# Graph convolutions and first experts: products wait for the tile or half of the columns they read, not for the whole stage before

## The chip, the cores and the metric

One core of one Trainium2 chip runs the whole program. Its engines are TensorE (PE, matmuls into PSUM banks, with weight loads PEld beside them), VectorE (DVE), ScalarE (ACT), GpSimd (POOL) and SyncE (SP, which issues transfers). Each runs its own list of instructions in order, and they wait for one another through counting semaphores. The metric is the device time of one execution in microseconds.

## What is computed

A two-layer network of a graph and token mixture: 625 nodes with 768 features, 20,000 edges. The change touches two parts of layer 0: two graph convolutions, and a mixture of eight small experts with the two best chosen for each node.

```python
# graph convolution, twice (a relu between)
h = x @ W
out = segment_sum(h[src] * (dinv[src] * dinv[dst])[:, None], dst) + b
# first experts: hidden width 192 each, top 2 of 8
hidden = gelu(einsum("ecd,edh->ech", padded, w1) + b1, approximate=False)
out    = einsum("ech,ehd->ecd", hidden, w2) + b2
final  = zeros.at[pt].add(out[se, pos] * pw[:, None])
```

Behind them come an attention of a second kind, a graph attention and the large experts, which the change doesn't touch.

## The kernel before, in words

**Precision.** Every float32 product is made of three matmuls (`mm3`, lines 341 to 343): an operand is a pair of an upper half, which ScalarE makes (`upper`, line 359), and a lower half, which VectorE makes from it (`lower`, line 362). Each pair counts on a semaphore once its lower half is there. So a stage hands over like this: TensorE fills a bank, ScalarE reads it and writes the upper half, VectorE writes the lower half, and TensorE may read the pair.

**Sizes.** The 625 nodes stand in `TT` = 5 tiles of `P` = 128; `D` = 768 columns are `KD` = 6 blocks of 128, and two halves of `HALF` = 384. Where nodes are the columns of a product they are cut into `SPANS` = (0, 320) and (320, 306).

**Banks.** `ring.next(...)` hands out the eight PSUM banks in turn, and makes TensorE wait for the eviction of what stood in that bank eight products earlier.

**Graph convolutions** (`graph_convolutions`). The edges have been counted into a dense matrix `adj` of 625 x 625. Per layer TensorE makes

- ten *node products* `node(layer, n)` with `c, t = divmod(n, TT)`: tile t of x times column half c of W, six terms, 18 matmuls of 384 columns. The result is the pair `h`; its lower half counts on `h_lo` ("node_lo"). All five tiles of half 0 come before those of half 1;
- in layer 1 twelve *neighbour products*, m over six blocks of 128 columns of h and s over the two spans: five terms, 15 matmuls of 320 or 306 columns. ScalarE adds bias and relu, and the pair goes to `xT`, counted on `z_lo` ("hidden_lo");
- in layer 2 ten *sums*, tile t outside and half c inside, 15 matmuls of 384 columns each, which VectorE adds to x. After tile t VectorE and ScalarE normalise it, and TensorE transposes tile t - 1 (`turn_tensor`).

The matrix `adj` itself is scaled tile by tile during the node products of layer 1; its lower halves count on `adj_lo`.

**First experts** (`dense_experts`). The hidden layer of all experts (1536) is made in two halves kh of twelve *hidden units*, each one block of 128 hidden numbers by one span: units 0 to 2 of a half are span 0 of its first three blocks, 3 to 5 span 1 of them, 6 to 8 span 0 of the last three blocks, 9 to 11 span 1. With each unit goes a short product of two matmuls, the gates' rows (lines 354 and 355). ScalarE applies gelu, VectorE multiplies by the gate, ScalarE and VectorE split the result into the pair `hT`, counted on `h_lo` ("hidden_lo"). Then come ten *sums* over the six blocks: 21 matmuls each in half 0 (with a bias term), 18 in half 1. In half 0 all tiles of c = 0 come first, in half 1 tile t stands outside and c inside.

At each of the five hand-overs TensorE had one wait for the last lower half of the stage:

```python
pe.wait_ge(*h_lo.at(2 * TT))        # before the neighbour products
pe.wait_ge(*z_lo.at(2 * KD))        # before the node products of layer 2
pe.wait_ge(*h_lo.at(4 * TT))        # before the sums
pe.wait_ge(*h_lo.at(12 * (kh + 1))) # experts: before the sums of each half
```

Of the kernel before, what the change touches and what calls it, by code (L numbers as in the profile page):

```python
# [17 lines left out]
P = 128  # L18
T = 625
TT = (T + P - 1) // P  # L20
# [4 lines left out]
KD = D // P  # L25
HALF = D // 2
# [36 lines left out]
SPANS = [(0, 320), (320, 306)]  # L63
# [7 lines left out]
class Signal:  # L71
# [20 lines left out]
    def at(self, n):  # L92
        return self.semaphore, self.base + n
# [48 lines left out]
def tok(t):  # L142
    return slice(t * P, (t + 1) * P)
# [11 lines left out]
def program(nc, ins, out, slots_dram, ctx):  # L155
    pe, act, dve, pool, sp = nc.tensor, nc.scalar, nc.vector, nc.gpsimd, nc.sync
# [95 lines left out]
    def buffers(i):  # L252

        n = width[i]
        if slot[i] == DEPTH:
            return tuple(part[:, 0:n] for part in fifth)
        return raw[:, slot[i], 0:n], whi[:, slot[i], 0:n], wlo[:, slot[i], 0:n]
# [74 lines left out]
    def weight(*key):  # L332

        i = place[key]
        pe.wait_ge(w_lo.semaphore, i + 1)
        k = TERMS.get(key[0], KD)
        return tuple(w.rearrange("p (k n) -> p k n", k=k) for w in buffers(i)[1:])
# [646 lines left out]
    def graph_convolutions(xT_ready):  # L984
# [24 lines left out]
        def tensor():  # L1009
            def node(layer, n):  # L1010
                c, t = divmod(n, TT)
                w = weight(f"gnn0_w{layer}", c)
                bank = ring.next(h_lo.at(2 * TT * (layer - 1) + n + 1))
                h_banks.append(bank)
                product(bank[:, 0:HALF], [(at(xT, ALL, k, tok(t)), at(w, ALL, k, ALL)) for k in range(KD)]).then_inc(*h_full.one())

            pe.wait_ge(*xT_ready)
            for n in range(4):
                node(1, n)
            pe.wait_ge(*adj_lo.at(1))  # L1020
            pe.wait_ge(*ones_made.now())
            for i, (a0, n) in enumerate(((0, 320), (320, 320))):
                bank = ring.next(deg_kept.at(i + 1))
                deg_banks.append(bank)
                product_exact_a(bank[0:E, 0:n], [(ones[:, 0:E], at(adj, ALL, k, slice(a0, a0 + n))) for k in range(TT)]).then_inc(*deg_full.one())
            node(1, 4)
            pe.wait_ge(*deg_kept.at(2))
            bank = ring.next(deg_root.at(1))
            deg_banks.append(bank)
            for t in range(TT):  # L1030
                end = pe.transpose(bank[:, t * E:(t + 1) * E], deg_row[:, tok(t)], ident[0:E, 0:E])
            end.then_inc(*deg_full.one())
            node(1, 5)
            pe.wait_ge(*deg_inv.at(1))
            for i, (t0, n) in enumerate(SPREAD):
                bank = ring.next(looped.at(2 * TT))
                deg_banks.append(bank)
                for k in range(n):
                    end = pe.transpose(bank[:, k * P:(k + 1) * P], deg_col[:, t0 + k:t0 + k + 1].broadcast_to([P, P]), ident[:, :])
                end.then_inc(*deg_full.one())  # L1040
            for n in range(6, 2 * TT):
                node(1, n)
            pe.wait_ge(*h_lo.at(2 * TT))
            pe.wait_ge(*adj_lo.at(1 + TT))
            for m in range(KD):
                for s, (a0, n) in enumerate(SPANS):
                    bank = ring.next(z_relu.at(2 * m + s + 1))
                    z_banks.append(bank)
                    product(bank[:, 0:n], [(at(h, ALL, k, slice(m * P, (m + 1) * P)), at(adj, ALL, k, slice(a0, a0 + n)))
                                           for k in range(TT)]).then_inc(*z_full.one())  # L1050
            pe.wait_ge(*z_lo.at(2 * KD))
            for n in range(2 * TT):
                node(2, n)
            pe.wait_ge(*h_lo.at(4 * TT))
            for t in range(TT):
                for c in range(2):
                    bank = ring.next(y_added.at(2 * t + c + 1))
                    y_banks.append(bank)
                    product(bank[:, 0:HALF], [(at(adj, ALL, k, tok(t)), at(h, ALL, k, slice(c * HALF, (c + 1) * HALF)))
                                              for k in range(TT)]).then_inc(*y_full.one())  # L1060
                if t > 0:
                    norm.turn_tensor(t - 1)
# [189 lines left out]
    def dense_experts(norm, x_ready):  # L1252
# [9 lines left out]
        m = sb("ffn0_m", [P, 2, TT], F32, scope)  # L1262
# [52 lines left out]
        def tensor():  # L1315
            def logits():
                pe.wait_ge(*gate_lo.at(1))
                pe.wait_ge(*xT_ready[-1])
                for s, (a0, n) in enumerate(LOGIT_SPANS):
                    bank = ring.next(logits_kept.at(s + 1))  # L1320
                    logit_banks.append(bank)
                    product(bank[0:E, 0:n], [(at(gp, ALL, k, ALL), at(xT, ALL, k, slice(a0, a0 + n))) for k in range(KD)]).then_inc(*logits_full.one())

            def logits_turned():
                pe.wait_ge(*logits_kept.at(2))
                bank = ring.next(logits_kept.at(3))
                logit_banks.append(bank)
                for t in range(TT):
                    end = pe.transpose(bank[:, t * E:(t + 1) * E], logit_rows[:, tok(t)], ident[0:E, 0:E])
                end.then_inc(*logits_full.one())  # L1330

            def counts_turned():
                pe.wait_ge(*count_f_made.at(TT))
                for t in range(TT):
                    for k0, kn in PARTS:
                        bank = ring.next(count_kept.at(len(count_banks) + 1))
                        count_banks.append(bank)
                        for k in range(kn):
                            end = pe.transpose(bank[:, k * P:(k + 1) * P], count_f[:, k0 + k, tok(t)], ident[:, :])
                        end.then_inc(*count_turned.one())  # L1340

            def hidden(i):
                hid, _, span, n = unit(i)
                w = weight("ffn0_w1", i // 6)
                pe.wait_ge(*xT_ready[-1 if i % 6 // 3 else (SPANS[0][1] - 1) // P])
                bank = ring.next(gelu.at(i + 1))
                hid_banks.append(bank)
                mm = hid % 3
                product(bank[:, 0:n], [(at(w, ALL, k, slice(mm * P, (mm + 1) * P)), at(xT, ALL, k, span)) for k in range(KD)]).then_inc(*hid_full.one())

            def picked(i):
                hid, _, span, n = unit(i)
                bank = ring.next(gated.at(i + 1))
                pick_banks.append(bank)
                product_exact_a(bank[:, 0:n], [(sel[:, hid, :], at(gT, ALL, span))]).then_inc(*pick_full.one())

            hidden(0)
            norm.turn_tensor(TT - 1)
            hidden(1)
            hidden(2)  # L1360
            logits()
            hidden(3)
            logits_turned()
            hidden(4)
            hidden(5)
            counts_turned()
            gates_tensor(gates, gate_banks)
            hidden(6)
            pe.wait_ge(*gT_lo_made.at(TT))
            pe.wait_ge(*sel_made.at(1))  # L1370
            for i in range(EARLY):
                picked(i)
            for kh in range(2):
                for i in range(max(EARLY, 12 * kh), 12 * (kh + 1)):
                    hidden(i)
                    picked(i)
                pe.wait_ge(*h_lo.at(12 * (kh + 1)))
                pe.wait_ge(*b2_lo.at(1))
                for i, (t, c) in enumerate(SUMS[kh]):
                    w = weight("ffn0_w2", 2 * kh + c)  # L1380
                    cols = slice(c * HALF, (c + 1) * HALF)
                    n = ROWS[t]
                    rows = slice(t * P, t * P + n)
                    bank = ring.next(y_added.at(2 * TT * kh + i + 1))
                    y_banks.append(bank)
                    terms = [(at(hT, ALL, k, rows), at(w, ALL, k, ALL)) for k in range(HK)]
                    if kh == 0:
                        terms.append((at(gT, ALL, rows), at(b2p, ALL, cols)))
                    product(bank[0:n, 0:HALF], terms).then_inc(*y_full.one())
                    if kh == 1 and c == 1 and t > 0:  # L1390
                        norm2.turn_tensor(t - 1)
# [1985 lines left out]
```

## Time and profile before

| | us |
|---|---|
| median of 3 runs | 1967.06 (1966.3 to 1967.81) |
| the profiled execution | 1970.35 |
| its span | 1968.5 |
| TensorE busy with matmuls | 1850.9 (94% of the span) |
| VectorE busy | 1292.1 (66%) |
| ScalarE busy | 934.7 (47%) |
| layer 0's graph convolutions, in the span | about 313 to 438 |
| its experts, in the span | about 438 to 605 |

Times in the rows are microseconds from the start of the span. TensorE's matmuls are pipelined: the time between two starts is what a matmul costs, not its duration, which is longer. The granted clock of TensorE is a share of 2.4 GHz; 0.50 is its lower level, 1.2 GHz. Idle time of an engine is followed by the instruction whose end released it. The chain of work that ended last runs over TensorE for nearly all of its length that is put down to an engine (43% of the span against 3% for VectorE).

### The profile page before, as it was taken

How to read it: one execution, taken by the hardware profiler on the slowest of the kernel's cores; microseconds unless marked ns; L12 is line 12 of the kernel's file. 1: busy time of each engine (PE TensorE's matmuls, PEld its weight loads, DVE VectorE, ACT ScalarE, POOL GpSimd, SP SyncE). 2: the span in 40 equal slices, each digit the busy share in tenths (PEclk: the TensorE clock that was granted, in tenths of full speed). 3: DMA queues.
4: the chain of work that ended last, by engine and by line, in shares of the span. 5: the costliest groups of instructions: out<-in, count | busy, mean ns of one | idle time of the engine just before them, and what ended most of it. 6: DMA issues, size and time to landing. Idle time of an engine off the chain costs nothing.

```text
span 1968.5 us, 30877 instructions
## 1 busy us (share of the span) xinstructions
PE 1850.9 (94%) x12157; PEld 1753.9 (89%) x12158; DVE 1292.1 (66%) x2489; ACT 934.7 (47%) x1547; POOL 150.5 (8%) x127
## 2 busy tenths in 40 slices
PE   6987999999999999788789999999999999999998
PEld 5876789998899999787689999999999999999998
DVE  7997766555245556888865754456566667676886
ACT  2331223315125435878534232345555566666776
POOL 0000000003000022333100000000101001001010
PEclk9997999999999989899799999999999999999999
DMA  3110002101113112010131132255656567677795
GB/s 117 49 49 1 25 25 105 54 6 71 49 49 110 54 36 95 22 38 17 64 123 61 62 105 73 73 208 181 220 193 221 214 217 242 219 260 250 282 318 203
DMA packets 36844, 234.30 MB, mean 119 GB/s; under 512 B 5964, under 2 KB 7366, under 8 KB 14680
## 3 DMA queue, kind: packets, MB, share of 16 engines
q1 hardware_dynamic: 31366, 217.41, 31.1%
q0 software_dynamic: 2656, 8.99, 2.1%
q10 hardware_dynamic: 2674, 5.87, 0.8%
q8 instruction: 99, 1.62, 0.3%
q14 instruction: 49, 0.40, 0.1%
HBM read 221.91 MB, written 10.35 MB: 118 GB/s over the span
## 4 chain that ended last, share of the span: by engine, by line
PE 43%; issue 3%; DVE 3%; DMA 1%; ACT 1%; POOL 0%; ACTq 0%; POOLq 0%; DVEq 0%
PE bank L2755 8%; PE bank L341 7%; PE bank L342 7%; PE bank L343 7%; PE bank L2756 4%; PE bank L2767 3%; PE bank L2771 2%; PE bank L2759 2%; PE bank L2768 2%; PE bank L2770 1%; PE bank L2758 1%; DVE weight_lo L314 1%; DMA out<-ffn_y,slot_token 0%; PE bank L2713 0%; DMA weight_raw_fifth<-in_ffn_w 0%
## 5 line engine op out<-in xcount | busy, mean ns | idle before, releaser
L314 DVE TENSOR_TENSOR weight_lo<-weight_raw,weight_hi 128x2304 fp32r<-128x2304 f32 (+1 forms) x155 | 392.3, 2536 | 51.5 <-ACT weight_hi L304 51.4
L304 ACT ACTIVATE weight_hi<-weight_raw 128x2304 fp32r<-128x2304 f32 (+1 forms) x155 | 323.3, 2087 | 76.7 <-DMA weight_raw<-in_ffn_w 55.0
L341 PE MATMUL bank<-xT_hi,weight_hi 128*128 128x320 f32 (+1 forms) x576 | 183.2, 318 | 5.3 <-DVE xT_lo L362 5.2
L342 PE MATMUL bank<-xT_lo,weight_hi 128*128 128x320 f32 (+1 forms) x576 | 178.3, 310 | 0.0
L343 PE MATMUL bank<-xT_hi,weight_lo 128*128 128x320 f32 (+1 forms) x576 | 178.1, 309 | 0.0
L341 PE MATMUL bank<-weight_hi,xT_hi 128*128 128x384 f32 (+1 forms) x480 | 161.2, 336 | 11.2 <-DVE weight_lo L314 6.2
L3135 DVE TENSOR_TENSOR hidden_tmp<-hidden_tmp,bank 128x160 f32<-128x160 f32 (+5 forms) x192 | 65.6, 342 | 160.7 <-ACT hidden_tmp L2918 160.7
L342 PE MATMUL bank<-weight_lo,xT_hi 128*128 128x384 f32 (+1 forms) x480 | 157.0, 327 | 0.0
L343 PE MATMUL bank<-weight_hi,xT_lo 128*128 128x384 f32 (+1 forms) x480 | 156.7, 326 | 0.0
L613 PE MATMUL bank<-one_hot_dst,one_hot_src 125*128 125x313 f16 x800 | 123.5, 306 | 15.2 <-ACT packed_counts L627 7.9
L2918 ACT ACTIVATE hidden_tmp<-bank,ffn_b_by_load 128x160 f32<-128x160 f32 (+5 forms) x192 | 73.3, 402 | 117.5 <-PE bank L2759 112.8
L341 PE MATMUL bank<-weight_hi,hidden_hi 128*128 128x384 f32 (+1 forms) x366 | 124.6, 340 | 0.5 <-DVE weight_lo L314 0.5
L342 PE MATMUL bank<-weight_lo,hidden_hi 128*128 128x384 f32 (+1 forms) x366 | 123.8, 338 | 0.0
L613 PEld LDWEIGHTS bank<-one_hot_dst,one_hot_src 125*128 125x128 f16 x800 | 75.0, 100 | 52.4 <-DVE one_hot_dst L585 17.2
L2755 PE MATMUL bank<-xT_hi,weight_hi 128*128 128x512 f32 (+3 forms) x390 | 117.4, 361 | 3.4 <-DVE xT_lo L3090 1.7
L341 PEld LDWEIGHTS bank<-xT_hi,weight_hi 128*128 128x128 f32 x576 | 110.3, 192 | 10.6 <-issue 7.7
L343 PE MATMUL bank<-weight_hi,hidden_lo 128*128 128x384 f32 (+1 forms) x348 | 117.7, 338 | 0.0
L2755 PE MATMUL bank<-xT_lo,weight_hi 128*128 128x320 f32 (+3 forms) x390 | 110.5, 350 | 5.6 <-DVE xT_hi L3090 4.6
L342 PEld LDWEIGHTS bank<-xT_lo,weight_hi 128*128 128x128 f32 x576 | 110.6, 192 | 0.0
L343 PEld LDWEIGHTS bank<-xT_hi,weight_lo 128*128 128x128 f32 x576 | 110.4, 192 | 0.0
L341 PEld LDWEIGHTS bank<-weight_hi,xT_hi 128*128 128x128 f32 x480 | 93.1, 194 | 13.5 <-DVE weight_lo L314 7.0
L2756 PE MATMUL bank<-xT_hi,weight_lo 128*128 128x256 f32 (+3 forms) x390 | 97.7, 250 | 0.0
(495 smaller groups left out, 5040.8 us busy)
## 6 DMA issues: line engine op xcount, KB each, us to landing
weight_raw<-in_ffn_w SPq DMA_DIRECT2D x111, 1152.0 KB, 5.2
weight_raw_fifth<-in_ffn_w SPq DMA_DIRECT2D x25, 1152.0 KB, 5.2
weight_raw<-in_shared_w SPq DMA_DIRECT2D x16, 1152.0 KB, 5.1
weight_raw<-in_mix_kv SPq DMA_DIRECT2D x8, 1152.0 KB, 7.0
weight_raw<-in_gat_w SPq DMA_DIRECT2D x8, 768.0 KB, 4.3
weight_raw<-in_mix_q SPq DMA_DIRECT2D x4, 1152.0 KB, 5.1
weight_raw<-in_mix_out SPq DMA_DIRECT2D x4, 1152.0 KB, 5.2
weight_raw<-in_gnn_w SPq DMA_DIRECT2D x4, 1152.0 KB, 5.6
```

The costliest lines, as they stand in the source:

```text
L304: act.activation(upper_, whole_, ACT.Copy).then_inc(*w_hi.one())
L314: dve.tensor_tensor(lower_, whole_, upper_.bitcast(F32), ALU.subtract).then_inc(*w_lo.one())
L341: pe.matmul(dst, a[0], b[0], start=first, stop=False)
L342: pe.matmul(dst, a[0], b[1], start=False, stop=False)
L343: return pe.matmul(dst, a[1], b[0], start=False, stop=last)
L613: end = pe.matmul(edge_banks[t][:, 0:TM], hot_src[:, j % HOT, tok(t)], hot_dst[:, j % HOT, 0:TM], start=(i == 0), stop=(i == CHUNK_E - 1))
L2755: pe.matmul(both, hi[:, k, :], x_e[:, k, :, 0:width], start=(k == 0), stop=False)
L2756: pe.matmul(first, lo[:, k, :], x_e[:, k, 0, 0:width], start=False, stop=False)
L2759: end = pe.matmul(both, hi[:, k, :], x_e[:, k, :, 0:width], start=False, stop=True)
L2767: pe.matmul(both, hi[:, k, :], h[:, k, :, 0:width], start=(first and k == 0), stop=False)
L2918: act.activation(ht[:, i % 3, 0:CAPS[e]], r_banks[i][:, 0:CAPS[e]], ACT.Identity, bias=b1r[:, e, i % (3 * NCH):i % (3 * NCH) + 1]).then_in ...
L3135: dve.tensor_tensor(part, part, r_banks[i][:, width:2 * width], ALU.add).then_inc(*r_sum.one())
```

## The change

Five single waits become waits at the head of each product, on the count that this product's operands need:

```diff
@@ graph convolutions
-            pe.wait_ge(*h_lo.at(2 * TT))
             pe.wait_ge(*adj_lo.at(1 + TT))
             for m in range(KD):
+                pe.wait_ge(*h_lo.at(TT if (m + 1) * P <= HALF else 2 * TT))
                 for s, (a0, n) in enumerate(SPANS):
...
-            pe.wait_ge(*z_lo.at(2 * KD))
             for n in range(2 * TT):
+                pe.wait_ge(*z_lo.at(2 * KD - 1 if (n % TT + 1) * P <= SPANS[0][1] else 2 * KD))
                 node(2, n)
-            pe.wait_ge(*h_lo.at(4 * TT))
             for t in range(TT):
                 for c in range(2):
+                    pe.wait_ge(*h_lo.at((3 + c) * TT))
                     bank = ring.next(y_added.at(2 * t + c + 1))
...
@@ first experts
-                pe.wait_ge(*h_lo.at(12 * (kh + 1)))
                 pe.wait_ge(*b2_lo.at(1))
                 for i, (t, c) in enumerate(SUMS[kh]):
+                    pe.wait_ge(*h_lo.at(12 * kh + (9 if (t + 1) * P <= SPANS[0][1] else 12)))
                     w = weight("ffn0_w2", 2 * kh + c)
```

So the neighbour products of column blocks 0 to 2 ask for the node products of half 0 alone; node tiles 0 and 1 of layer 2, which lie inside the first span of 320, ask for step 11 of 12; the sums of half 0 of the columns ask for 15 of 20 node products; the experts' sums of tiles 0 and 1 ask for nine of twelve units.

No instruction moves on any engine. TensorE's matmuls stand in the same order, and 34 heads of products have one more wait. On TensorE, at the head of the third neighbour product (bank free of `deg` work: "loops_added"; "node_lo" is `h_lo`):

```order
 L342 MATMUL bank<-adj_lo,gcn_h_hi 128x306
 L343 MATMUL bank<-adj_hi,gcn_h_lo 128x306
-L341 MATMUL bank<-adj_hi,gcn_h_hi 128x320 [waits loops_added]
+L341 MATMUL bank<-adj_hi,gcn_h_hi 128x320 [waits loops_added,node_lo]
 L342 MATMUL bank<-adj_lo,gcn_h_hi 128x320
 L343 MATMUL bank<-adj_hi,gcn_h_lo 128x320
```

The first product's head has the same names before and after, with a lower count behind "node_lo"; the third has the wait anew. On TensorE, at the head of the experts' second sum of half 0 ("hidden_gated" is the bank's eviction, "weight_lo_made" the weights', "hidden_lo" the wait on `h_lo`):

```order
 L342 MATMUL bank<-ffn_b_lo,ffn_gatesT_hi 8x384
 L343 MATMUL bank<-ffn_b_hi,ffn_gatesT_lo 8x384
-L341 MATMUL bank<-weight_hi,ffn_hT_hi 128x384 [waits hidden_gated,weight_lo_made]
+L341 MATMUL bank<-weight_hi,ffn_hT_hi 128x384 [waits hidden_gated,weight_lo_made,hidden_lo]
 L342 MATMUL bank<-weight_lo,ffn_hT_hi 128x384
 L343 MATMUL bank<-weight_hi,ffn_hT_lo 128x384
```

A head that had two waits has three; the matmuls around it stand where they stood.

## Rows read from the trace of the kernel before

**Rows 1.** The page's first part: busy us, share of span, instructions.

```profile
PE 1850.9 (94%) x12157; PEld 1753.9 (89%) x12158; DVE 1292.1 (66%) x2489; ACT 934.7 (47%) x1547; POOL 150.5 (8%) x127
```

**Rows 2.** Waits of TensorE, whole span: us in total, times, longest.

```profile
PE bank L341 <- DVE ffn_hT_lo L362: 4.5, 2, 2.8
```

**Rows 3.** Timeline, TensorE, hand-over 1: start, duration, instruction, idle before.

```profile
344.53 0.34 PE L343 MATMUL bank<-weight_hi,xT_lo 128*128 128x384 f32 x1
346.04 0.42 PE L341 MATMUL bank<-adj_hi,gcn_h_hi 128*128 128x320 f32 x1 [1.17 <-DVE gcn_h_lo L362]
346.29 0.31 PE L342 MATMUL bank<-adj_lo,gcn_h_hi 128*128 128x320 f32 x1
```

**Rows 4.** Timeline, TensorE, hand-over 2.

```profile
371.89 0.30 PE L343 MATMUL bank<-adj_hi,gcn_h_lo 128*128 128x306 f32 x1
373.79 0.44 PE L341 MATMUL bank<-weight_hi,xT_hi 128*128 128x384 f32 x1 [1.61 <-DVE xT_lo L362]
```

**Rows 5.** Timeline, TensorE, hand-over 3, and the first transposes behind it.

```profile
404.76 0.33 PE L342 MATMUL bank<-weight_lo,xT_hi 128*128 128x384 f32 x1
404.93 0.34 PE L343 MATMUL bank<-weight_hi,xT_lo 128*128 128x384 f32 x1
406.44 0.45 PE L341 MATMUL bank<-gcn_h_hi,adj_hi 128*128 128x384 f32 x1 [1.17 <-DVE gcn_h_lo L362]
406.72 0.34 PE L342 MATMUL bank<-gcn_h_lo,adj_hi 128*128 128x384 f32 x1
...
416.96 0.81 PE L474 MATMUL bank<-identity,counts_with_loops 128*128 128x128 f32 x6
```

**Rows 6.** Stretches: us, busy of PE, PEld, DVE, ACT, POOL, clock, DMA, GB/s.

```profile
484.00:488.00 4.00, 2.70 (x9) 2.70 (x10) 1.94 (x3) 3.22 (x3) 0.00 (x0) 0.71 0.61 256
700.00:1100.00 400.00, 349.63 (x2258) 332.78 (x2257) 294.57 (x840) 232.41 (x470) 82.80 (x73) 0.91 0.16 56
```

**Rows 7.** Timeline, VectorE, before hand-over 1: the last tile of `adj_lo`.

```profile
342.93 0.82 DVE L362 TENSOR_TENSOR adj_lo<-counts_with_loops,adj_hi 128x640 fp32r<-128x640 f32 x1
```

**Rows 8.** Timeline, VectorE, before hand-over 2: step 11 of 12.

```profile
371.17 0.49 DVE L362 TENSOR_TENSOR xT_lo<-gcn_tmp,xT_hi 128x320 fp32r<-128x320 f32 x1 [0.87 <-ACT xT_hi L359]
```

**Rows 9.** Timeline, VectorE, behind hand-over 3: tile 0 normalised.

```profile
414.46 0.68 DVE L466 TENSOR_SCALAR counts_with_loops<-x,ln_moments,ln_rstd 128x768 f32<-128x768 f32 x1
```

**Rows 10.** Timeline, TensorE, hand-over 4, experts' first half.

```profile
479.03 0.30 PE L355 MATMUL bank<-ffn_gatesT_lo,expert_rows_r 8*128 8x306 f32 x1
479.26 0.41 PE L341 MATMUL bank<-xT_hi,weight_hi 128*128 128x306 f32 x1
479.50 0.30 PE L342 MATMUL bank<-xT_lo,weight_hi 128*128 128x306 f32 x1
...
482.23 0.30 PE L355 MATMUL bank<-ffn_gatesT_lo,expert_rows_r 8*128 8x306 f32 x1
485.30 0.44 PE L341 MATMUL bank<-weight_hi,ffn_hT_hi 128*128 128x384 f32 x1 [2.77 <-DVE ffn_hT_lo L362]
485.58 0.45 PE L342 MATMUL bank<-weight_lo,ffn_hT_hi 128*128 128x384 f32 x1
...
489.03 0.36 PE L341 MATMUL bank<-weight_hi,ffn_hT_hi 128*128 128x384 f32 x1
```

**Rows 11.** Timeline, VectorE, before hand-over 4: units 9 and 12.

```profile
480.38 0.49 DVE L362 TENSOR_TENSOR ffn_hT_lo<-ffn_acted,ffn_hT_hi 128x320 fp32r<-128x320 f32 x1 [0.61 <-ACT ffn_hT_hi L359]
...
484.77 0.48 DVE L362 TENSOR_TENSOR ffn_hT_lo<-ffn_acted,ffn_hT_hi 128x306 fp32r<-128x306 f32 x1 [0.59 <-ACT ffn_hT_hi L359]
```

**Rows 12.** Timeline, TensorE, hand-over 5, experts' second half.

```profile
566.54 0.30 PE L355 MATMUL bank<-ffn_gatesT_lo,expert_rows_r 8*128 8x306 f32 x1
568.56 0.44 PE L341 MATMUL bank<-weight_hi,ffn_hT_hi 128*128 128x384 f32 x1 [1.71 <-DVE ffn_hT_lo L362]
```

**Rows 13.** Timeline, VectorE, before hand-over 5: unit 21.

```profile
558.43 0.49 DVE L362 TENSOR_TENSOR ffn_hT_lo<-ffn_acted,ffn_hT_hi 128x320 fp32r<-128x320 f32 x1 [0.61 <-ACT ffn_hT_hi L359]
```

**Rows 14.** Waits between 300 and 450 us: ScalarE for TensorE's banks.

```profile
ACT gcn_tmp L1099 <- PE bank L343: 11.1, 10, 1.2
```

## The prediction

> **What bounds the kernel now.** I read the busy line first: TensorE holds 94% of the span [rows 1], so time can come only from its idle stretches or from a slower clock inside its busy ones. Next the waits of TensorE: the two hand-overs of the first experts cost it 4.5 us [rows 2], and the same kind of wait stands at three hand-overs of the graph convolutions (1.17, 1.61 and 1.17 us in [rows 3 to 5]). In all five the row reads the same way: TensorE sits idle, released by VectorE's last low half of the stage before (`gcn_h_lo`, `xT_lo`, `gcn_h_lo`, `ffn_hT_lo` twice), and then starts a product whose own operands had long been there. The rows of VectorE around them say when each operand was there. Last the granted clock: it is at 0.71 of full in 484 to 488 us [rows 6], right behind the longest of the five waits.
>
> **Part by part: how long each hand-over takes now and what is left.** I measure from the start of the last matmul of the old stage to the start of the second of the new one, since the first after a pause starts slowly. Matmuls of 384 columns follow each other every 0.17 us [rows 5], those of 320 columns then every 0.15 us (0.17 x 320/384).
>
> 1. Node products to neighbour products (layer 1). 344.53 to 346.29, 1.76 us [rows 3]. The first six products need only the first half of the columns of h (done with node 5 of 10) and all of `adj_lo`, whose last tile ends at 342.93 + 0.82 = 343.75 [rows 7], before TensorE is free at 344.70. Left: 0.17 + 0.15 = 0.32. Gain 1.44 us. The second half, ready at 346.0 as now, is first needed six products later (some 13 us): covered.
> 2. Neighbour products to node products (layer 2). 371.89 to 373.79 is 1.90 [rows 4], and 0.28 to the second matmul, as behind wait 3, which has the same shape [rows 5]: 2.18 us. Node tiles 0 and 1 need VectorE's step 11 of 12, which ends at 371.17 + 0.49 = 371.66 [rows 8]; TensorE is free at 372.04. Left: 0.15 + 0.17 = 0.32. Gain 1.86 us. Step 12 is there when TensorE now resumes, 373.8; tile 2 asks for it after two node products of 18 x 0.17 = 3.1 us, at 378: covered.
> 3. Node products to sums (layer 2). 404.93 to 406.72, 1.79 us [rows 5], left 0.35: gain 1.44 us. The first sum needs only the half c = 0, made five nodes (15 us) before; the second starts 15 x 0.17 = 2.6 us later, at 407.7, and its operand is there at 406.4: covered, by 1.3 us, the thinnest cover of the five. What is late next: the transposes of tile 0 (416.96 now [rows 5]) move to 415.5, and want VectorE's normalisation of that tile, which ends at 414.46 + 0.68 = 415.14 even if VectorE moves by nothing [rows 9].
> 4. Hidden units to sums, first half of the experts. 482.23 to 485.58, 3.35 us [rows 10]. Behind the short gate-row product, a product starts after 0.23 and its second matmul after 0.24 (479.03, 479.26, 479.50 [rows 10]): left 0.47, gain 2.88 us. Tiles 0 and 1 need unit 9, which ends at 480.38 + 0.49 = 480.87 [rows 11], 1.5 us before TensorE is free. Unit 12 ends at 484.77 + 0.48 = 485.25 [rows 11]; tile 2 asks for it after two sums of 21 x 0.17 = 3.6 us each, at 489.7: covered.
> 5. The same, second half. 566.54 to 568.56 is 2.02 [rows 12], plus 0.28: 2.30; left 0.47, gain 1.83 us. Unit 21, which is now enough, ends at 558.43 + 0.49 = 558.92 [rows 13]; tile 2 comes four sums (12 us) later.
>
> Sum of the five: 1.44 + 1.86 + 1.44 + 2.88 + 1.83 = 9.45 us. The idle rows alone (1.17 + 1.61 + 1.17 + 2.77 + 1.71 = 8.4) are its lower bound.
>
> **The clock.** Behind wait 4 the matmuls of 384 columns fall to the lower of TensorE's two levels, 1.2 instead of 2.4 GHz: eleven steps, 485.58 to 489.03, take 3.45 us [rows 10] where 11 x 0.175 = 1.9 would do. With 2.77 us of idle gone, nothing is left in front of this stretch that the trace shows ahead of a fall, so I add 1.5 us. Its bounds are 0 and 1.6. Together 9.45 + 1.5 = 11.0 us. The Trainium skill ("TensorE: Matmul & The Clock Gate", section "HAM oscillation — how this bites in real kernels") puts such falls down to idle stretches between bursts of matmuls; by that rule, too, the fall goes with the wait, and the trace agrees (0.71 behind the wait of 2.77 us).
>
> **What is added.** The heads of 34 products get one wait more, on a count that is already reached; matmuls, their order and all other engines' instructions are the same. Behind those waits the rest of TensorE's queue stands, and behind that everybody. A head with two waits (bank free, weights ready) inside the node products carries no gap: the products run on at 0.17 us, as ten products fill 373.79 to 405.10 in 31.3 us, which is 180 x 0.174 [rows 4, 5]. I cost the third wait at nothing; bounds: 0, and 0.17 us a head, a whole step (5.8 us for 34). I take 0, the row of the same kind. The Trainium skill ("Perfetto Trace Analysis", section "Identifying Dependency Chains") warns against this change here: instructions that wait on several engines may get extra semaphore instructions in front. It gives no price; with it at a whole step a head the sum would be 5.2 us, and the rows of two-wait heads speak against that.
>
> **Does the gain reach the end?** ScalarE waits for TensorE's bank before 10 of the neighbour products' evictions, 11.1 us in all [rows 14], so both helpers have slack in stage 2 and follow an earlier TensorE. The same holds for the sums, where VectorE waits for TensorE. The weights' loads are issued when TensorE has read the old ones, so they move with it. After 600 us nothing is anchored to the clock on the wall: each stage starts from the one before. I carry the full 11.0 us to the end.
>
> **Rivals.**
> - *The fall of the clock stays or lands elsewhere near by.* Then 9.45 us: 1957.6. For it: the lower level set in only when matmuls ran again, after 485.58 [rows 10], so pause and fall are not one event. Against: no other pause stands near it.
> - *The later falls shift.* Between 700 and 1100 us the clock is at 0.91 in the mean [rows 6]: 0.09 x 2 x 400 = 72 us at the lower level, costing up to 36 us. These stretches come 11 us earlier now, and if the clock's monitor meets them otherwise, 10% more or less of them is 3.6 us either way: 1952.5 or 1959.7. The three timed runs lie within 1.5 us, which speaks for small changes. The same page of the Trainium skill (section "What's actually happening") calls the monitor's window free-running, not reset when a kernel starts; no row here can show that, and it would make this change one of luck.
> - *The change doesn't do what it says* at one hand-over: an earlier operand is late after all. At wait 3, with 1.3 us of cover, or wait 2, with 0.4, it would give back at most that gain: 1957.5 to 1958.
> - *Helpers catch up instead.* A later stage that ScalarE and VectorE bound swallows part of the 11: 1960 to 1966. Against: they start from TensorE's products there too.
> - *Slower: the third wait.* Place: the 34 heads. It decides from 11.0 / 34 = 0.32 us a head; at 0.5 us each it costs 17 and the kernel runs at 1973. Against: two waits cost nothing measurable.
>
> **How the numbers follow.** The profiled execution took 1970.35 us around its span of 1968.5, 3.3 above the median of 1967.06; absolute terms carry over: 1967.06 - 11.0 = **1956.1 us**. Chances: forecast as worked out, 1954.5 to 1957.5, 0.62; fall stays or one term smaller, 1957.5 to 1959, 0.14; later falls shift, 0.14, half each way; a helper swallows part or no gain worth the name, 0.07; slower 0.03. The range 1952 to 1961 leaves out under 0.15: the slower case, most of the swallowed gain and the far ends of the shifted falls. A measurement of this kernel tells 0.2% (3.9 us) from no change. Faster by more than that needs under 1963.1: 0.92; within it 0.05; slower 0.03.
>
> **What would show it.** In the profile after: no wait of TensorE for `gcn_h_lo` or `ffn_hT_lo` (2.3 and 4.5 us now), that for `xT_lo` down by 1.6; a clock of 1.00 through the first sums of the experts; ScalarE's and VectorE's busy times unchanged. Wrong would be a step that shows a wait with another name at one of the five places; the cover, if tile 2 of the experts waits for `ffn_hT_lo`; the cost of waits, if gaps of "issue" stand at the heads; and the carry to the end, if the 600 to 1968 us stretch takes longer than before.

## The result, and the profile after

The changed kernel takes **1956.76 us** (median of 4, 1954.79 to 1957.77) against 1967.43 us (median of 4, 1966.3 to 1970.49): ratio 0.994, 95% interval 0.9928 to 0.9952, some 11 us less. Forecast were 1956.1 us, with 1952 to 1961. The profiled execution took 1956.79 us around a span of 1954.8, against 1970.35 and 1968.5.

First the page of the kernel after: the span, then the busy line that answers to [rows 1].

```profile
span 1954.8 us, 30891 instructions
PE 1847.9 (95%) x12157; PEld 1753.5 (90%) x12158; DVE 1292.1 (66%) x2489; ACT 935.6 (48%) x1547; POOL 151.3 (8%) x127
```

As many matmuls as before, VectorE's and ScalarE's work unchanged. Next the waits of TensorE over the whole span (us in total, times, longest). The entry of [rows 2] has no answer in it: there is no wait for `ffn_hT_lo` or `gcn_h_lo` any more, and that for `xT_lo` has gone from 6.8 us in three to

```profile
PE bank L341 <- DVE xT_lo L362: 5.2, 2, 3.7
```

The timeline of TensorE at the five hand-overs of the kernel after (start, duration, instruction); they answer to [rows 3, 4, 5, 10, 12]:

```profile
344.78 0.34 PE L343 MATMUL bank<-weight_hi,xT_lo 128*128 128x384 f32 x1
344.95 0.31 PE L341 MATMUL bank<-adj_hi,gcn_h_hi 128*128 128x320 f32 x1
345.10 0.31 PE L342 MATMUL bank<-adj_lo,gcn_h_hi 128*128 128x320 f32 x1
...
370.69 0.30 PE L343 MATMUL bank<-adj_hi,gcn_h_lo 128*128 128x306 f32 x1
370.83 0.34 PE L341 MATMUL bank<-weight_hi,xT_hi 128*128 128x384 f32 x1
371.01 0.33 PE L342 MATMUL bank<-weight_lo,xT_hi 128*128 128x384 f32 x1
...
401.89 0.34 PE L343 MATMUL bank<-weight_hi,xT_lo 128*128 128x384 f32 x1
402.06 0.34 PE L341 MATMUL bank<-gcn_h_hi,adj_hi 128*128 128x384 f32 x1
402.24 0.34 PE L342 MATMUL bank<-gcn_h_lo,adj_hi 128*128 128x384 f32 x1
...
479.28 0.30 PE L355 MATMUL bank<-ffn_gatesT_lo,expert_rows_r 8*128 8x306 f32 x1
479.52 0.44 PE L341 MATMUL bank<-weight_hi,ffn_hT_hi 128*128 128x384 f32 x1
479.80 0.34 PE L342 MATMUL bank<-weight_lo,ffn_hT_hi 128*128 128x384 f32 x1
...
559.24 0.30 PE L355 MATMUL bank<-ffn_gatesT_lo,expert_rows_r 8*128 8x306 f32 x1
559.47 0.44 PE L341 MATMUL bank<-weight_hi,ffn_hT_hi 128*128 128x384 f32 x1
559.75 0.34 PE L342 MATMUL bank<-weight_lo,ffn_hT_hi 128*128 128x384 f32 x1
```

No row has an idle entry. The new stage follows the old one after 0.17, 0.14, 0.17, 0.24 and 0.23 us, the first of the two steps that the prediction left in its sum.

To see where 13.7 us of span went, take the start of the same matmul in both traces and subtract. This table is worked out that way; a column is a place in the kernel before, a number is how much later (+) or earlier (-) that matmul starts there than in the first profile of the kernel before.

```
start before:    344    347    375    408    461    481    486.5  490    527    570    625    700    730    1110   1955
after           +0.25  -1.19  -3.04  -4.49  -4.47  -2.94  -6.29  -7.31  -7.31  -9.09  -9.09  -9.09 -13.93 -13.32 -14.00
```

The shift of 0.25 us at 344 is there before the first changed wait: it comes from the first 300 us, where such shifts differ from execution to execution. Then there are five steps down at the five hand-overs, but one step **up**, +1.53 us between 461 and 481, where nothing was changed; and one more down at 700 to 730, where nothing was changed either. The first is in this piece of the same timeline, behind the seven early gate-row products:

```profile
461.35 0.30 PE L354 MATMUL bank<-ffn_gatesT_hi,expert_rows_r 8*128 8x320 f32 x1
461.50 0.30 PE L355 MATMUL bank<-ffn_gatesT_lo,expert_rows_r 8*128 8x320 f32 x1
461.73 0.41 PE L341 MATMUL bank<-xT_hi,weight_hi 128*128 128x320 f32 x1
461.98 0.31 PE L342 MATMUL bank<-xT_lo,weight_hi 128*128 128x320 f32 x1
462.13 0.39 PE L343 MATMUL bank<-xT_hi,weight_lo 128*128 128x320 f32 x1
462.32 0.47 PE L341 MATMUL bank<-xT_hi,weight_hi 128*128 128x320 f32 x1
...
465.25 0.47 PE L343 MATMUL bank<-xT_hi,weight_lo 128*128 128x320 f32 x1
465.52 0.35 PE L341 MATMUL bank<-xT_hi,weight_hi 128*128 128x320 f32 x1
```

From 462.32 to 465.52 twelve steps are 0.27 us long in place of 0.15: TensorE at its lower level, 1.2 GHz. The stretches say the same (us, busy of PE, PEld, DVE, ACT, POOL, then the clock, DMA share, GB/s); the last one is where the fall of [rows 6] stood in the kernel before, and it is at full clock now:

```profile
456.00:460.00 4.00, 3.90 (x26) 3.27 (x24) 1.48 (x6) 4.00 (x11) 2.70 (x2) 1.00 0.41 173
458.00:462.00 4.00, 4.00 (x27) 3.62 (x27) 2.42 (x4) 2.43 (x3) 4.00 (x3) 1.00 0.01 2
461.00:465.00 4.00, 4.00 (x20) 3.81 (x19) 3.09 (x4) 0.74 (x2) 4.00 (x3) 0.65 0.00 0
478.00:482.00 4.00, 4.00 (x24) 3.63 (x24) 1.68 (x4) 2.77 (x4) 0.00 (x0) 1.00 0.47 152
```

So the fall behind hand-over 4 did go, and an equal one came some 20 us earlier in the order of work. The step at 700 to 730 is a fall that stood in the first profile of the kernel before and not in that of the kernel after. Of the kernel before, then of the kernel after, where the same matmuls start 9 us earlier and more:

```profile
716.00:720.00 4.00, 4.00 (x21) 4.00 (x20) 2.72 (x7) 0.00 (x0) 0.00 (x0) 0.50 0.00 0
720.00:724.00 4.00, 4.00 (x21) 4.00 (x21) 1.51 (x4) 0.00 (x0) 0.30 (x1) 0.50 0.00 0
```

```profile
708.00:712.00 4.00, 4.00 (x38) 4.00 (x37) 2.89 (x9) 0.00 (x0) 0.68 (x2) 1.00 0.00 0
```

### The profile page after: what moved, and what is told of

Same layout as the page of the kernel before. It is cut to its first block, busy times and chain, and to the rows that moved or that the text cites. A ratio compares the mean times of both kernels' runs of the same rounds, so it can differ in the third digit from the quotient of the medians.

```text
span 1954.8 us, 30891 instructions
## 1 busy us (share of the span) xinstructions
PE 1847.9 (95%) x12157; PEld 1753.5 (90%) x12158; DVE 1292.1 (66%) x2489; ACT 935.6 (48%) x1547; POOL 151.3 (8%) x127
## 4 chain that ended last, share of the span: by engine, by line
PE 44%; issue 3%; DVE 3%; ACT 1%; DMA 1%; POOL 0%; ACTq 0%; POOLq 0%; DVEq 0%
PE bank L2755 8%; PE bank L341 7%; PE bank L342 7%; PE bank L343 7%; PE bank L2756 4%; PE bank L2767 3%; PE bank L2771 2%; PE bank L2759 2%; PE bank L2768 2%; PE bank L2770 1%; PE bank L2758 1%; DVE weight_lo L314 1%; PE bank L2713 0%; DMA weight_raw_fifth<-in_ffn_w 0%; DMA out<-ffn_y,slot_token 0%
## 5 line engine op out<-in xcount | busy, mean ns | idle before, releaser
L341 PEld LDWEIGHTS bank<-weight_hi,xT_hi 128*128 128x128 f32 x480 | 93.5, 195 | 11.6 <-DVE weight_lo L314 7.0
```

Source lines behind the costliest of these rows:

```text
L341: pe.matmul(dst, a[0], b[0], start=first, stop=False)
```

## The experiments

Two things had to be told apart. Do the falls of the clock belong to a kernel (same place in every execution), or do they wander? And what do hand-overs, falls and waits cost, each by itself? All ratios are to the kernel before on the same chip.

### The two kernels again

No edit.

> The changed kernel once more, unaltered. Theory A (falls of the clock wander): the handovers give 9.45 us in every execution, while the falls of TensorE's clock come at other places in another execution of the same kernel. Then the five handovers stand gap-free again, but the low stretch of 462.3 to 465.5 us (behind the seven early gate-row products) need not be there, and the one of 713 to 724 us may be back; the mean clock of 700 to 1100 us differs from that of the first profile by 0.005 or more. Time against before: 9.5 us less, give or take 1.5. Theory B (falls belong to the kernel's own order of work): low stretch again in 462 to 466, none around 711, mean clock of 700 to 1100 as in the first profile; time 11 to 14 us less than before.

Measured: 1954.94 us (median of 6 executions), ratio 0.9931, interval 0.9916 to 0.9946; that is 14.2 us less by the medians and 13.6 by the ratio. The low stretch behind the early gate-row products is there again, the one around 711 is not, as theory B has it. But the mean clock of 700 to 1100 us differs by more than 0.005, as theory A has it (from the clock's own records 0.915 in the first profile, 0.923 in this one). Of this second profile of the kernel after:

```profile
462.00:466.00 4.00, 4.00 (x18) 4.00 (x18) 2.78 (x5) 0.94 (x2) 4.00 (x3) 0.57 0.00 0
700.00:1100.00 400.00, 350.79 (x2265) 333.05 (x2265) 297.76 (x843) 232.50 (x467) 82.89 (x73) 0.92 0.17 59
```

> The kernel before once more, unaltered. Theory A: its falls wander too, so that the low stretch of 485.6 to 489.0 us behind the wait of 2.8 us may be missing, and another may stand behind the seven early gate-row products (466 to 470 us). Theory B: the low stretch behind the wait of handover 4 is there again, and the one of 714 to 724.5 us too, at the same places within 0.5 us. Both: the five waits of 1.17, 1.61, 1.17, 2.77 and 1.71 us again, within 0.05.

Measured: one execution, 1969.1 us. The rows below belong to this second profile of the kernel before: the fall behind hand-over 4 is back at its place, but the one at 714 to 724 is gone, though nothing differs. The five waits are as long as before.

```profile
462.00:466.00 4.00, 4.00 (x27) 3.62 (x26) 2.42 (x4) 2.51 (x3) 4.00 (x2) 1.00 0.01 2
484.00:488.00 4.00, 3.07 (x10) 3.07 (x11) 2.15 (x2) 3.53 (x3) 0.00 (x0) 0.64 0.52 221
716.00:720.00 4.00, 4.00 (x38) 4.00 (x38) 3.56 (x11) 0.00 (x0) 0.12 (x1) 1.00 0.00 0
700.00:1100.00 400.00, 351.68 (x2257) 336.76 (x2257) 293.91 (x840) 232.16 (x470) 82.66 (x73) 0.90 0.16 56
```

By the table's method this execution gained 4.85 us at 730 and had lost them again by 1000, in longer low stretches elsewhere. What follows: each theory holds in one region. From 200 to 620 us the falls of a kernel stand at the same place in its order of work in every profile, within 0.7 us; behind 700 us some come in one execution and not in the next.

### The two halves of the change apart

The diff's experts' hunk alone:

> The change at the experts' two handovers alone; the three of the graph convolutions as before. The prediction's sum: 2.88 + 1.83 = 4.71 us less, plus 1.5 if the fall behind handover 4 goes with the wait in every execution (theory B: 6.2), plus nothing in the mean if falls wander (theory A: 4.7). In the trace: handovers 4 and 5 without an idle row, 1 to 3 with 1.17, 1.61, 1.17.

Measured: 1959.86 us, ratio 0.9956 (0.9943 to 0.9969). Up to 625 us it gained 6.1 us (2.83 and 1.78 at the hand-overs, 1.5 from the fall that went): theory B's number in this profile, and no fall behind the gate-row products. Of its profile:

```profile
464.00:468.00 4.00, 4.00 (x28) 3.81 (x27) 3.39 (x3) 0.77 (x2) 4.00 (x2) 1.00 0.01 2
482.00:486.00 4.00, 4.00 (x22) 3.51 (x22) 1.47 (x4) 3.25 (x4) 0.00 (x0) 1.00 0.85 297
```

The diff's graph convolutions' hunks alone:

> The change at the three handovers of the graph convolutions alone; the experts as before. The prediction's sum: 1.44 + 1.86 + 1.44 = 4.74 us less. Both theories give that, save for what later falls add or take (up to 2 us either way). In the trace: no idle row at handovers 1 to 3; at handover 4 the wait of 2.77 us unchanged, since VectorE's chain moves with TensorE. The rival that a helper swallows part would show there as a longer wait at handover 4.

Measured: 1962.74 us, ratio 0.9971 (0.9961 to 0.9981). The three hand-overs gave 1.44, 1.85 and 1.45 us. But from 300 to 625 us only 2.7 of those 4.74 us were left. Of its profile, the waits of TensorE between 300 and 620 us, then three stretches:

```profile
PE bank L341 <- DVE ffn_hT_lo L362: 3.4, 2, 1.7
```

```profile
460.00:464.00 4.00, 4.00 (x17) 3.96 (x17) 2.79 (x5) 0.94 (x2) 4.00 (x3) 0.57 0.00 0
480.00:484.00 4.00, 4.00 (x17) 4.00 (x16) 2.97 (x2) 2.42 (x2) 0.00 (x0) 0.63 0.45 191
562.00:566.00 4.00, 3.11 (x10) 3.11 (x11) 2.18 (x2) 3.55 (x3) 0.00 (x0) 0.62 0.64 264
```

My expectation of an unchanged wait was wrong, and the reason is worth having: the new fall delayed TensorE by 1.54 us, but VectorE's chain, which releases hand-over 4, by nothing until its last unit and by 0.5 us there. So the wait shrank from 2.77 to 1.71 us and took 1.06 of the fall's price. Then the fall behind hand-over 4 came all the same, and another behind hand-over 5 (562 us), which the kernel before doesn't have, though its wait there is as long (1.71 us). So the length of a pause alone doesn't decide whether a fall comes. The parts are not additive: 6.1 and 2.7 apart, 9.35 together.

### Does the time of arrival make the fall behind the gate-row products?

The changed kernel, with TensorE delayed by busy work between hand-over 3 and the experts; the copies are overwritten:

```diff
+                    if (t, c) == (2, 0):
+                        for _ in range(2):
+                            product(bank[:, 0:HALF], [...])
                     product(bank[:, 0:HALF], [...]).then_inc(*y_full.one())
```

> The changed kernel with two useless copies of one sum (2 x 15 matmuls, 5.2 us) in the graph convolutions, behind handover 3: TensorE reaches the early gate-row products when it did in the kernel before (within 0.7 us). If the time of arrival decides on the fall behind them: no low stretch there, as in the kernel before and in the kernel with the experts' part alone, so the 5.2 us cost 3.7 up to 480 us. If the removed waits ahead decide: the low stretch stays and the delay costs its 5.2.

Measured in its one profile: the delay cost 5.2 us up to 461 us and 3.7 up to 481: no fall. Of this profile:

```profile
464.00:468.00 4.00, 4.00 (x29) 3.81 (x27) 3.39 (x3) 0.84 (x2) 4.00 (x2) 1.00 0.01 2
468.00:472.00 4.00, 4.00 (x26) 3.42 (x25) 2.66 (x6) 1.03 (x3) 4.00 (x3) 1.00 0.00 0
```

In full: 1961.36 us, ratio 0.9967 (0.9953 to 0.9981), against 1956.44 and 0.9941 of the changed kernel beside it: 4.9 us more by the medians. The profile has a fall at 709 us, which those of the changed kernel have not, so the 3.7 us of this stage are read from the profile alone. Arrival decides, here, and not the removed waits, as far as one profile can say. Over all profiled executions with the same order of work there: first gate-row product at 457.7 to 460.0 us, fall in 8 of 8; at 463.4 to 464.7 us, none in 5 of 5. Only the delayed kernel has the later arrival without the three waits ahead of it.

The start of the span is a rough ruler for an arrival. The clock's records begin at 19.9 us in one profile and at 22.5 in another, and the matmuls at 300 us are early or late in nearly the same order, from 1.6 us before those of the first profile of the kernel before to 0.8 behind. Counted from the last rise of the clock, at 194 to 197 us, the gate-row products with a fall begin after 263.4 to 264.1 us and those without after 268.3 to 269.4, so it may be the distance from the clock's own changes that counts. No run separates the two.

### Does the unbroken run of gate-row products make it?

```diff
             for i in range(EARLY):
+                if i == 3:
+                    hidden(EARLY)
                 picked(i)
...
-                    hidden(i)
+                    if i > EARLY:
+                        hidden(i)
```

The same is done on ScalarE.

> The changed kernel with hidden unit 7 (18 full matmuls, 2.6 us) put between the third and the fourth of the seven early gate-row products, on TensorE and ScalarE, so that 6 and then 10 matmuls of 8 rows follow one another instead of 14 and 2. Theory E (the fall behind the early products comes from their unbroken run): no low stretch there, 1.5 us less than the changed kernel up to 480 us. Theory F (the fall comes from where the kernel stands at that moment, whatever its order, or from the transposes ahead of it): the low stretch stays, at the same time, time as the changed kernel within 0.3 us in this stage. If it goes, the time behind it follows, save for later falls.

Measured: theory E. The gate-row products begin at 459.4 us, amid the arrivals that had the fall (263.8 us by the second ruler), and in its one profile there is none:

```profile
458.00:462.00 4.00, 4.00 (x26) 3.61 (x26) 2.42 (x3) 2.27 (x2) 4.00 (x3) 1.00 0.01 2
462.00:466.00 4.00, 4.00 (x27) 3.62 (x26) 2.79 (x6) 0.94 (x2) 4.00 (x2) 1.00 0.00 0
...
704.00:708.00 4.00, 4.00 (x22) 4.00 (x21) 3.40 (x7) 0.00 (x0) 0.00 (x0) 0.52 0.00 0
708.00:712.00 4.00, 4.00 (x21) 4.00 (x21) 1.82 (x5) 0.00 (x0) 0.00 (x0) 0.50 0.00 0
```

From 300 to 625 us it gains 10.9 us on the kernel before, 1.5 more than the changed kernel. But the two last rows, of the same profile, are the fall of 700 to 730 us again, and it costs 4.9. In full 1958.65 us, ratio 0.9949 (0.9931 to 0.9967) against 0.9941 (0.9922 to 0.9961): no better, as far as this can be told. Its executions spread from 1952.81 to 1960.61 us, and the profiled one is among the slow ones of them. A local gain of 1.5 us is less than what the later falls throw in or take.

### Are the later falls a matter of arrival too?

A pure delay in front of the third sum of the experts' second half:

```diff
+                    if kh == 1 and i == 2:
+                        for _ in range(3):      # 2, 1
+                            product(bank[0:n, 0:HALF], terms)
```

> The changed kernel with three useless copies of one product (3 x 18 matmuls, overwritten by the real one) put into the experts' second half, in front of its third sum: a pure delay of TensorE by 3 x 3.1 = 9.4 us with its array busy, so that everything from 620 us on starts when it did in the kernel before. Theory C (the later falls of the clock depend on when the stages behind 700 us start, counted from the kernel's start): the delay costs more than its own 9.4 us, some 13 to 14, and the kernel runs like the kernel before, about 1968; mean clock of 700 to 1110 us as in the kernel before. Theory D (nothing but the delay): 1955 + 9.4 = 1964.3, and half of the extra 4 us that the change brought beyond its handovers stays.

Measured: 1966.01 us (12 executions, 1963.17 to 1972.01), ratio 0.9987 (0.9974 to 1.0).

> The same with two useless copies, 6.2 us. Theory D: 1955 + 6.2 = 1961.2. Theory C: off that line by up to 4 us either way, as the stages behind 700 us meet the clock's monitor otherwise; the low stretches between 776 and 1080 us stand at other instructions or have other lengths than in the changed kernel.

Measured: 1962.55 us, ratio 0.9968 (0.9956 to 0.9981).

> The same with one useless copy, 3.1 us. Theory D: 1955 + 3.1 = 1958.1. Theory C: off that line by up to 4 us either way.

Measured: 1958.78 us, ratio 0.9949 (0.9931 to 0.9966).

> The kernel before with one useless copy at the same place, 3.1 us: everything behind 620 us starts 3.1 us later than in the kernel before. Theory D: 1969.1 + 3.1 = 1972.2. Theory C: off that line by up to 4 us; if the kernel before sits at an unlucky start of those stages, it costs less than 3.1, or even gains.

Measured: 1972.77 us, ratio 1.0015 (1.0 to 1.003).

Next to the changed kernel's 1954.94 us, measured on another chip, the delays of 3.1, 6.2 and 9.4 us cost 3.8, 7.6 and 11.1 us, and by the ratios against 0.9931 they cost 3.5, 7.3 and 11.0. Against its ratio of 0.9941 from a third chip they cost 1.6, 5.3 and 9.1, so the reference alone moves the answer by 2 us. The kernel before, delayed, took 1972.77 against 1970.08 us beside it, 2.7 for 3.1. That lies at D or between the theories, and the intervals let neither go. The profiles say more. What the stretch from 625 to 1955 us took, against the first profile of the kernel before (by the table's method), with the shift at which it began:

```
                     shift at 700   625 to 1955        shift at 700   625 to 1955
before                    0.0          0.0    experts_only    -6.7     -5.3
before_again             -0.4         -0.1    graph_only      -4.2     -5.2
after_plus9              +0.9         -0.8    after_plus6     -2.8     -5.1
before_plus3             +3.9         -1.1    delay_before..  -6.7     -2.7
after, again, ref  -9.1 -9.0 -10.0   -4.9 -5.4 -5.1
more_waits               -9.8         -5.6    after_plus3     -7.7     -1.3
spread_picks            -10.8         +0.1
```

The four executions that began this stretch within 0.4 us of the first profile or later took about as long as it (0.0 to 1.1 us less); eight of the ten earlier ones were faster, by 2.7 to 5.6 us, but two were not. And the profiled execution of the kernel with the delay of 9.4 us took 1970.82 us, 4.8 above its median, about the price of the one fall that it has at 715 us: its row need not be typical. So the rows suggest that timing has a say, and don't show it; a shift alone doesn't tell which falls will come.

### What a wait costs that is already fulfilled

```diff
+            def more_waits():
+                for ready in (adj_hi.at(1), deg_full.at(1), deg_inv.at(1)):
+                    pe.wait_ge(*ready)
```

called at the heads of the neighbour products, of layer 2's node products and of the sums, and three of the same kind at the experts' sums; beside it the changed kernel as the reference.

> The changed kernel with three more waits, on counts reached long before, at the head of each of the 52 products of the five stages (156 waits). Prediction's step (a reached wait costs nothing): same time as the changed kernel, the products run on at one matmul per 0.174 us across their heads. Rival (a wait costs a share of a step): at 0.17 us each, 26 us more; at 0.03 us each, 5 us more, seen as gaps at the heads.

> The changed kernel once more, beside the three below on the same chip. Low stretch of the clock behind the early gate-row products again, at the third or fourth matmul of the hidden unit behind them, 1.5 us lost there; time some 13 us under the kernel before, if the two earlier measurements (10.7 and 13.6) hold.

Measured: with the waits 1955.37 us, ratio 0.9937 (0.9913 to 0.9962); without 1956.44 us, ratio 0.9941 (0.9922 to 0.9961). The latter is 10.8 us under the kernel before by the medians, 11.6 by the ratio, less than the 13 I had expected; its fall behind the gate-row products is there again. The experts' first sum in the kernel with the added waits, which has seven in front of it, three of them added:

```profile
478.57 0.30 PE L355 MATMUL bank<-ffn_gatesT_lo,expert_rows_r 8*128 8x306 f32 x1
478.81 0.44 PE L341 MATMUL bank<-weight_hi,ffn_hT_hi 128*128 128x384 f32 x1
479.09 0.34 PE L342 MATMUL bank<-weight_lo,ffn_hT_hi 128*128 128x384 f32 x1
```

0.24 and 0.28 us, as in the kernel after. Up to 625 us the two kernels' gains are 9.33 and 9.36 us. The trace counts all 156 waits on TensorE, in 87 more semaphore instructions (642 against 555), and they cost nothing that can be seen; the slower rival needed 0.32 us for each of 34. It shows why, too: these instructions take 51 ns each in TensorE's sequencer, and those in front of the sum above stand at 476.00 to 476.22 us, 2.6 us ahead of its first matmul at 478.81, while the matmuls before it run.

## Why the prediction was right, and where it was not

**The five hand-overs** (1.44 + 1.86 + 1.44 + 2.88 + 1.83 = 9.45 us). Measured 1.44, 1.85, 1.45, 2.83 and 1.78: 9.35. Measuring from the last start of the old stage to the second start of the new one was the right ruler: the idle entries alone gave 8.4. The fourth and fifth terms are 0.05 too large: the second matmul of the new stage comes after 0.28 us behind a gate-row product even without a pause (479.52 to 479.80, 559.47 to 559.75), where the sum left 0.24.

**The covers.** All five held. The experts' tile 2 never waited for its last part; no wait under another name came up at the five places.

**The clock** (+1.5 us). The price was right (1.53 us at that place, and the fall went in the kernel after and in the experts' half), the step "nothing is left in front" was wrong as a sum over the stage. TensorE, arriving 4.5 us earlier, now has a fall behind the fourteen 8-row matmuls, at 1.5 us; the prediction had looked for a pause in front of a fall and had no term for one without. The rival that the fall lands elsewhere near by (1957.6, chance 0.14 with a smaller term) is what happened: the fall is in all three profiles of the changed kernel, in that of its twin with more waits and in the three with a delay behind it. The stage gave 9.35, not 11.0. The rule that I took from the Trainium skill ("TensorE: Matmul & The Clock Gate", section "HAM oscillation — how this bites in real kernels"), that idle stretches between bursts make the falls, agrees with hand-over 4: a fall follows in all four profiles with a pause there and in none of the ten without. It doesn't cover the new fall, which stands behind stretches in which TensorE was busy for 3.90 and for all 4.00 of 4 us.

**The carry to the end.** No helper swallowed anything: behind 1110 us nothing is lost. But the stage from 700 to 1110 us gave more than was carried to it. 9.35 us up to 625 and a total of 10.7 to 14.2 (by the medians 10.7, 14.2 and 10.8, by the ratios 11.8, 13.6 and 11.6) leave 1 to 5 us, which the profiles put into later falls of the clock, the rival with a chance of 0.14. So the forecast of 1956.1 met 1956.76 with two terms off in opposite senses: 1.5 too much in the experts, 1 to 5 too little behind them. That the point came out within 1 us is luck; the five hand-overs and the range, which took both rivals in, are not. The three timed runs within 1.5 us, from which I had argued that later falls change little, were too few: over 31 executions the kernel before spreads from 1963 to 1975 us.

**The added waits.** Nothing, as costed. Their number was off: the trace counts 41 more waits on TensorE than before (806 against 765 on its semaphore instructions), not 34, so the slower rival decides from 11.0 / 41 = 0.27 us each. The sum doesn't change.

## What to carry to other kernels

Here a stage's one wait for its last operand moved to the heads of the products at no price that could be seen, since the first products really need less; what each hand-over gave is the time from the last start before the pause to the second behind it, minus two ordinary steps. On an engine that is 94% busy that gain reached the end, but the granted clock behind it did not stay as it was: arriving earlier can bring a fall or spare one, and a change worth a few microseconds has to be read stage by stage from several profiles, not from one total.

## What the runs showed of the hardware that I had not expected

- TensorE's clock fell with the engine busy for all of the 4 us before (458 to 462 us). Seven gate-row products, fourteen matmuls with 8 of 128 rows in 2.2 us, are followed by 3.2 us at 1.2 GHz in 8 of 8 profiled executions that reach them at 457.7 to 460.0 us, and in 0 of 5 that reach them at 463.4 to 464.7. With 18 full matmuls put in their middle the fall went, at an arrival of 459.4 us (one profile).
- A fall on TensorE can be half paid by a wait: in the kernel with the graph convolutions' part alone 1.06 of 1.54 us went into the wait behind it, since VectorE, which releases it, lost only 0.5.
- A pause of 1.71 us in front of the experts' second sums has no fall behind it in the three profiles of the kernel before, with and without a delay behind it, and one in the kernel with the graph convolutions' part alone.
- From 200 to 620 us falls repeat from profile to profile at the same place in the order of work; from 700 us on not all do. The one at 714 to 724 us costs 4.85 us when it comes, and one execution of the kernel before had it and the other had not. What decides on it stays open: the shift of the stage's start alone doesn't order the cases.
